# Causal phase attention on one core: all-pairs score tiles against diagonal tiles with a running state for the first 128 keys

## The reference, cut to what matters

```python
key_ph = jnp.exp(1j * key_phase).reshape(Bx, Lx, N_SETS, PLANES)
qry_ph = jnp.exp(1j * query_phase).reshape(Bx, Lx, N_SETS, PLANES)
for s in range(N_SETS):
    bound = key_ph[:, :, s, :, None] * V[:, :, None, :]
    memory = jnp.cumsum(bound, axis=1)
    retrieved = (memory * jnp.conj(qry_ph[:, :, s, :, None])).sum(axis=2).real
    total = total + weights[s] * retrieved
```

## Time and profile before

| | us |
|---|---|
| median of 3 runs | 1647.76 (1645.76 to 1649.63) |
| the profiled execution's own time | 1646.93 |
| span of the profiled execution, first to last instruction | 1644.2 |
| PE busy in the span | 1455.5 (89%) |
| DVE busy | 1432.7 (87%) |
| ACT busy | 1246.3 (76%) |
| POOL busy | 1012.6 (62%) |

### The profile page before, as it was taken

How to read it: one execution, slowest core, us unless ns; L and a number is a source line. 1 busy time by engine, 2 the same in 40 slices (tenths; PEclk the granted TensorE clock), 3 DMA queues, 4 the chain that set the end, 5 groups by cost and what they waited for, 6 DMA issues and landing times.

```text
span 1644.2 us, 30506 instructions
## 1 busy us (share of the span) xinstructions
PE 1455.5 (89%) x9030; PEld 1121.5 (68%) x9030; DVE 1432.7 (87%) x5763; ACT 1246.3 (76%) x2190; POOL 1012.6 (62%) x857
## 2 busy tenths in 40 slices
PE   2689999999999999999999999999999972776671
PEld 1467777777777777777777777777777751555551
DVE  3369999999999999999999999999999983886661
ACT  2799999999999999999999999999999741111110
POOL 0116666666666666666666666666666665788887
PEclk9899999999999999999999999999999996998885
DMA  9977777777777777777677777777776102676653
GB/s 170 245 157 151 147 145 145 141 143 133 129 124 127 123 121 120 121 123 116 120 120 120 117 117 119 119 121 121 117 119 113 39 19 65 101 117 105 94 82 34
DMA packets 257947, 195.67 MB, mean 119 GB/s; under 512 B 59000, under 2 KB 237275, under 8 KB 257784
## 3 DMA queue, kind: packets, MB, share of 16 engines
q1 hardware_dynamic: 216280, 175.30, 59.6%
q0 software_dynamic: 39296, 17.55, 8.7%
q10 hardware_dynamic: 2208, 0.89, 0.4%
HBM read 84.28 MB, written 83.73 MB: 102 GB/s over the span
## 4 chain that ended last, share of the span: by engine, by line
PE 75%; POOL 10%; issue 5%; DVE 4%; DMA 3%; ACT 3%; SPq 1%; POOLq 0%; DVEq 0%
PE bank L896 12%; POOL out_rows L640 9%; PE bank L966 8%; PE bank L949 7%; PE bank L1037 6%; PE bank L1046 5%; PE bank L920 5%; PE bank L934 4%; PE bank L904 4%; PE bank L1053 3%; PE bank L1022 2%; PE bank L985 2%; PE bank L1012 2%; PE bank L1008 2%; PE bank L1002 2%
## 5 line engine op out<-in xcount | busy, mean ns | idle before, releaser
L596 POOL DMA_INDIRECT slot_rows<-xs,slot x640 | 648.9, 1014 | 447.4 <-DVE slot L1382 278.0
L657 ACT ACTIVATE img<-img 84x980 f32<-84x980 f32 x190 | 340.5, 1793 | 13.7 <-DMA img<-in_x 7.1
L896 PE MATMUL bank<-img,w_tok 126*128 126x392 f32 (+1 forms) x640 | 228.1, 504 | 29.2 <-DMA img<-img 23.7
L640 POOL DMA_INDIRECT out_rows<-img,etok x128 | 198.7, 1552 | 54.9 <-issue 36.1
L580 POOL TENSOR_TENSOR rs<-ve,neg_half 128x12 f32<-128x12 f32 (+1 forms) x66 | 150.0, 2273 | 111.2 <-DVE ve L1265 111.2
L896 PEld LDWEIGHTS bank<-img,w_tok 126*128 126x128 f32 (+1 forms) x640 | 124.0, 195 | 115.2 <-issue 23.9
L949 PEld LDWEIGHTS bank<-pos_a,v 128*128 128x128 f32 x768 | 139.8, 190 | 42.6
L727 ACT ACTIVATE xs<-h,nb,rs 128x128 f32<-128x128 f32 x384 | 154.1, 481 | 2.5 <-DVE nb L1271 2.5
L949 PE MATMUL bank<-pos_a,v 128*128 128x325 f32 (+2 forms) x768 | 155.7, 338 | 0.0
L740 ACT ACTIVATE xh<-h,nb,rs 128x128 f32<-128x128 f32 x384 | 154.0, 480 | 0.6 <-DVE nb L1271 0.6
L966 PE MATMUL bank<-a_t,v 128*128 128x325 f32 (+2 forms) x768 | 150.3, 345 | 0.6 <-DVE a_t L1325 0.6
(11 more groups left out here) (196 smaller groups left out, 3581.6 us busy)
## 6 DMA issues: line engine op xcount, KB each, us to landing
img<-in_x SPq DMA_DIRECT2D x384, 150.1 KB
img<-img SPq DMA_DIRECT2D x254, 160.8 KB
img<-img SPq DMA_DIRECT2D x128, 128.6 KB
out_rows<-fin SPq DMA_DIRECT2D x128, 128.0 KB
slot_rows<-xs,slot POOLq DMA_INDIRECT x640
slot_rows<-init_rows SPq DMA_DIRECT2D x16, 540.0 KB, 8.9
img<-slot_rows SPq DMA_DIRECT2D x32, 270.0 KB
h<-in_txt SPq DMA_DIRECT2D x64, 128.0 KB
```

The costliest lines, as they stand in the source:

```text
L596: g.indirect_dma_start(out=slots_d, out_offset=bass.IndirectOffsetOnAxis(ap=slot[0:nt, q.x, part, r:r + 1], axis=0), in_=xs[0:nt, q.x, par ...
L640: g.indirect_dma_start(out=out, out_offset=bass.IndirectOffsetOnAxis(ap=etok[:, q.load, m:m + 1], axis=0), in_=ysum[:, q.load, m, :], in_o ...
L657: a.activation(cols[:, b0:b0 + nb, :], raw[:, q.u, :].rearrange("p (t b) -> p b t", b=P)[:, b0:b0 + nb, :], ACT.Copy)\
L896: ins = mm(bank[:, 5, 0:2 * PATCHES], w_tok[r, m, :], xk[r, k.u, :, m, :], start=(m == 0), stop=(m == SHIFT - 1))
```

## The change: what it does, and the diff

Scores are kept for the diagonal blocks and the short last one: key tile 0 against queries 0 to 127, key tile 1 against queries 128 to 324, tile 2 against queries 256 to 324, that is 128, 197 and 69 columns (394 in one bank) for 325, 197 and 69 (591 in two). What the first 128 keys give to queries 128 to 324 comes through a state: PE transposes the keys' features of both samples in one operation (`keys`, bank 7), ACT copies them to `kt` (`key_rows`), PE multiplies them with the first values tile (`first_state`, two matmuls of 128 columns with 64 output partitions each, bank 2), ACT copies the state (`state_rows`), DVE scales the queries with the norm (`scaled_queries`, 197 columns), and `phase_out` adds state times scaled queries (two matmuls of 197 columns, contraction over 64 partitions). `phase_out` is now one function for both samples. The masks become one DVE operation of 394 columns per sample. The constants grow by 394 + 197 columns.

```diff
+SCORES = [(0, TILE), (TILE, L), (2 * TILE, L)]
+AT = [0, TILE, L, L + BELOW[2]]
...
+            def key_rows(y):
+                act.wait_ge(S["pe_kt"], y.count())
+                a.activation(kt[:, :], bank[:, 7, 0:TILE], ACT.Copy).then_inc(S["a_kt"], 1)
+            def state_rows(y):
+                act.wait_ge(S["pe_st"], y.count())
+                a.activation(state[:, :], bank[:, 2, 0:D], ACT.Copy).then_inc(S["a_st"], 1)
...
                     if not early(n1, 1):
                         turn_columns_1(n1)
+                if p2.runs():
+                    key_rows(p2)
                 if p1.runs():
                     normal_1(p1)
+                if p2.runs():
+                    state_rows(p2)
                 if p3.runs():
                     normal_2(p3)
...
-            def scores(y):
+            def keys(y):
                 pe.wait_ge(S["a_qs"], y.count())
                 pe.wait_ge(S["v_w"], y.count())
+                tr(bank[:, 7, 0:TILE], kq[:, y.u, 0, 0:TILE], ident).then_inc(S["pe_kt"], 1)
+            def scores(y):
                 wait(pe, S["a_sl"], y, 2)
                 for i, (t0, _) in enumerate(TILES):
                     for s in range(2):
                         r = slice(64 * s, 64 * s + 64)
-                        b = (6, 1)[s]
-                        at = 0 if i < 2 else BELOW[1]
-                        dst = bank[:, b + (i > 0), at:at + BELOW[i]]
-                        ins = mm(dst, kq[r, y.u, 0, t0:t0 + TILE], kq[r, y.u, 1, i * TILE:L], start=(i < 2), stop=(i != 1),
-                                 skip_group_check=True)
+                        a0, a1 = SCORES[i]
+                        ins = mm(bank[:, (6, 1)[s], AT[i]:AT[i + 1]], kq[r, y.u, 0, t0:t0 + TILE], kq[r, y.u, 1, a0:a1],
+                                 start=(i == 0), stop=(i == NT - 1), skip_group_check=True)
                 ins.then_inc(S["pe_sc"], 1)
+            def first_state(y):
+                pe.wait_ge(S["a_kt"], y.count())
+                for s in range(2):
+                    ins = mm(bank[64 * s:64 * s + 64, 2, 0:D], kt[:, 64 * s:64 * s + 64], v[:, y.u, s, 0, :], start=True, stop=True)
+                ins.then_inc(S["pe_st"], 1)
...
+            def phase_out(y):
                 pe.wait_ge(S["v_ma"], y.count())
-                phase_out(y, 0)
-            def phase_out_1(y):
-                phase_out(y, 1)
+                for s in range(2):
+                    flat = a_t[:, s].rearrange("p a l -> p (a l)")
+                    for i in range(NT):
+                        a0, a1 = SCORES[i]
+                        mm(bank[:, 6 + s, a0:a1], v[:, y.u, s, i, :], flat[:, AT[i]:AT[i + 1]],
+                           start=(i == 0), stop=False, skip_group_check=True)
+                pe.wait_ge(S["a_st"], y.count())
+                for s in range(2):
+                    r = slice(64 * s, 64 * s + 64)
+                    ins = mm(bank[:, 6 + s, TILE:L], state[r, :], qn[r, :], start=False, stop=True, skip_group_check=True)
+                ins.then_inc(S["pe_ta"], 1)
...
                 pe.wait_ge(S["a_xh"], k.count())
                 wait(pe, S["v_mb"], k, 1)
+                wait(pe, S["a_st"], k, 1)
...
                 if p2.runs():
+                    keys(p2)
                     scores(p2)
                 if p4.runs():
                     counts(p4)
+                if p2.runs():
+                    first_state(p2)
+                if p4.runs():
                     shared_out(p4)
...
+            def scaled_queries(y):
+                dve.wait_ge(S["a_qs"], y.count())
+                TT(qn[:, :], kq[:, y.u, 1, TILE:L], cst("norm"), ALU.mult)
             def mask(y, s, done, b):
-                TT(a_t[:, s, 0, :], bank[:, b, 0:L], cst("maskn")[:, 0:L], ALU.mult)
-                n = BELOW[1] + BELOW[2]
-                TT(a_t[:, s, 1, 0:n], bank[:, b + 1, 0:n], cst("maskn")[:, L:], ALU.mult).then_inc(S[done], 1)
+                flat = a_t[:, s].rearrange("p a l -> p (a l)")
+                TT(flat[:, 0:AT[NT]], bank[:, b, 0:AT[NT]], cst("maskp"), ALU.mult).then_inc(S[done], 1)
...
                 if p2.runs():
                     residual_bias(p2)
+                    scaled_queries(p2)
```

More of the change, by code:

```diff
@@ L66 @@
 for _n, _w in (("ident", 128), ("pos", L), ("tok", 2 * NT), ("sel", SETS), ("query", 1), ("key", 1), ("delta", 2), ("dpos", 1),
-               ("dump", 4), ("empty", 8), ("absent", 2 * NT), ("below", 128), ("maskn", BEGIN[NT]), ("iota", CAP)):
+               ("dump", 4), ("empty", 8), ("absent", 2 * NT), ("below", 128), ("maskn", BEGIN[NT]), ("maskp", AT[NT]), ("norm", BELOW[1]),
+               ("iota", CAP)):
     CONST[_n] = (_at, _at + _w)
@@ L95, in constants @@
     put("maskn", mask * n)
+    put("maskp", np.concatenate([m0[:, 0:TILE], m1, m2], 1) * np.concatenate([invn[:, a:b] for a, b in SCORES], 1))
+    put("norm", np.repeat(invn[:, TILE:L], 128, 0))
     put("iota", np.arange(CAP)[None, :])
@@ L284, in program @@
         kq = sb("kq", [128, 2, 3, L])
+        kt = sb("kt", [128, 128])
+        state = sb("state", [128, D])
+        qn = sb("qn", [128, BELOW[1]])
         v = sb("v", [128, 2, 2, NT, D])
@@ L379, in program @@
         s_spread = [sems(f"s_spread{n}") for n in range(COPIES)]
-        names = """pe_tok pe_th pe_tx pe_k pe_v pe_g pe_sc pe_pf pe_pa0 pe_pa1 pe_ta0 pe_ta1 pe_tx2 pe_f1a  pe_lgt  pe_f3b pe_lg pe_wo pe_o
+        names = """pe_tok pe_th pe_tx pe_k pe_v pe_g pe_kt pe_st pe_sc pe_pf pe_pa0 pe_pa1 pe_ta pe_tx2 pe_f1a  pe_lgt  pe_f3b pe_lg pe_wo pe_o
             v_ht  v_st1 v_mm v_dd v_vs v_ve v_nb v_v v_ma v_mb v_w v_u v_tot v_hb  v_h2 v_st2
@@ L383, in program @@
               v_sg  v_sinv
-            a_d0 a_d1 a_d2 a_h a_xh a_xt a_th a_abs a_sin a_qs a_g a_x2 a_x2t a_lgt a_sl a_lg a_small
+            a_d0 a_d1 a_d2 a_h a_xh a_xt a_th a_abs a_sin a_kt a_st a_qs a_g a_x2 a_x2t a_lgt a_sl a_lg a_small
             p_rs""".split()
@@ L960, in position_out_1 @@
                 position_out(y, 1)
[L962 to L970, removed]
-                pe.wait_ge(S["v_ma"], y.count())
-                phase_out(y, 0)
-            def phase_out_1(y):
-                phase_out(y, 1)
+            def phase_out(y):
+                pe.wait_ge(S["v_ma"], y.count())
+                for s in range(2):
[9 more added lines that the diff above has]
+                ins.then_inc(S["pe_ta"], 1)
             def transpose_2(z):
@@ L1089, in body @@
                 if p2.runs():
-                    phase_out_0(p2)
-                    phase_out_1(p2)
+                    phase_out(p2)
                 if p3.runs():
@@ L1396, in weigh_sets @@
             def weigh_sets(y):
-                dve.wait_ge(S["pe_ta1"], y.count())
+                dve.wait_ge(S["pe_ta"], y.count())
                 STT(gsets[:, :, :], gt[:, :, :], 1.0, bank[:, 6:8, 0:L], ALU.add, ALU.mult).then_inc(S["v_u"], 1)
```

## The result

The changed kernel takes 1674.78 us (median of 4, 1673.06 to 1676.72) against 1647.65 (median of 4 on the same chip): ratio 1.0165, 95% interval 1.0147 to 1.0182. It is slower by 1.65%; the forecast was 1673 us, range 1653 to 1688.

A forecast was written before the change was run, and what follows sets the result against it. PE's list was taken to bound the kernel at 20.00 us a turn; the five items sum to +0.41, so 1646.93 + 60 x 0.41 + 1 = 1672.5, forecast 1673 us with the median's offset, range 1653 to 1688.

The forecast's parts named there:

- PE is the ring: In the loop over pairs, PE's own list sets the 20.00 us turn; time added there counts about 60 times.
- Items 1 and 2: PE, per turn: key transpose of 128 columns +0.11 us; two score pair passes cut from 325 to 128 columns, -0.33.
- Item 3: PE, first_state: two pair passes of 128 columns, 0.22 us, in a new column-half block with edges 0.36; +0.58 a turn.
- Items 4 and 5: PE, phase_out: values times masked scores shortened, -0.65 us; state times queries in a new row-half block, +0.70 a turn.
- The loads in the open: At edges of half-array blocks on PE, weight loads start with their matmuls, not ahead; counted within the new edges' 0.73 us.
- rival A: New half-array blocks' weight loads are hidden, only emptying is paid: +0.03 us a turn, 1651 us; chance 0.08.
- Rival B: PE enters and leaves half-array blocks without emptying, only streaming counts: -0.32 us a turn, 1630 us; chance 0.07.
- Other engines: ACT's two copies, estimated 0.5 us, hidden by its waits for PE; DVE's products fall from 1.81 to 1.47 us, worth nothing.
- Rival C: New ACT wait at key_rows delays transpose_1 beyond 0.6 us to spare; 0.4 beyond gives +0.81 a turn, 1697 us; chance 0.06.
- Startup: Second constants DMA grows by 295.5 KB and delays the first images by 0 to 1.5 us; taken as 1 us.

The follow-up runs named there:

- third and fourth experiments: Changed kernel, order only: key transpose moved between score products, 1695.19 us; separately, first_state moved from behind the counts to right behind the scores, 1661.30 us.
- the reordered kernel: Changed kernel reordered: key transpose between token products, first_state right ahead of scores, state products right behind them, both copies on ACT; 1660.06 us, 1.0071 of the kernel before.

## Why the prediction was right

Steps by their place in the prediction:

- *PE is the ring.* Right. The turn grew from 20.00 to 20.42, forecast +0.41, while DVE's work got shorter and ACT's waits for PE stayed near 1.2 us a turn. The order-only runs (transpose inside the scores, `first_state` behind the scores) moved the time by +0.32 and -0.23 us a turn with every engine's work unchanged.
- *Items 1 and 2* (transpose, shorter scores): -0.18 for -0.22. *Item 3* (`first_state`): 0.57 for 0.58. *Items 4 and 5* together: +0.03 for +0.05. Prices read from existing blocks of the same operand shape carried over to blocks that the trace of before doesn't have.
- *The loads in the open.* The loads of L966 and L1005 start with their matmuls, and the sum with them in the open came out; rival A is out. The Trainium skill, "TensorE: Matmul & The Clock Gate", Part 2, has weight loads pulled ahead of running matmuls when they go to the background buffer or to other rows; the trace agrees in packed work (0.11 us ahead at L1000) and doesn't where the array's division changes (730.03 for 730.04, 734.46 for both). Rival B, beside which the prediction named the span model of the Trainium skill's "TensorE: Matmul & The Clock Gate", Part 3, is out by the third and fourth experiments (0.32 and 0.23 us for edges alone). The Trainium skill's "TensorEngine Tiling (Array Packing)", Key Properties, says that a change of tiling mode drains TensorE; these two runs agree.
- *Other engines.* Right: the masks took 0.557 us of DVE for 394 columns, the scaled queries 0.359 (forecast 0.56 and 0.35); the key copy on ACT started at 728.75, the state copy ended at 731.49, 0.79 us ahead of `transpose_1` at 732.28 (forecast 0.6). Rival C did not occur. DVE's busy time fell by 0.15 us a turn, less than these lengths give (0.34); it was worth nothing, as forecast. One reading was wrong without harm: the prediction took ACT's ring as its busy time, 18.75 + 0.5 us a turn, but a stretch of PE's list is part of that ring: it closes at 19.58 us without the copies and stopped the reordered kernel at 20.17. By it rival B's turn of some 19.7 could not have been reached with the copies on ACT.
- *Startup, forecast 1 us.* Wrong; no cost shows. The token products of the sixth and the last pair in the changed kernel:

```profile
132.68 3.46 PE L918 MATMUL bank<-img,w_tok 126*128 126x392 f32 x10
...
1318.11 3.46 PE L918 MATMUL bank<-img,w_tok 126*128 126x392 f32 x10
```

Before they stood at 132.46 and 1293.01. So with the larger constants the sixth pair is 0.2 us later (the DMA still landed in 12.1, and the first token products came 1.3 us earlier), 58 turns of 0.43 make 24.9, and from the last token products to the end are 353.2 us for 351.2, 2.0 that I had not foreseen. 0.2 + 24.9 + 2.0 = 27.1 is the difference of the spans. The 2.0 can't be put down to the change: the run with `first_state` behind the scores, which has the same work, took 350.9 us there, and the seven experiments lie between 350.3 and 354.4. That the total came so near the forecast is in part luck; the turn, 0.42 for 0.41, is not, though its parts missed by 0.04, 0.01 and 0.02 in directions that nearly cancel.

## What to carry to other kernels

On a packed PE count edges before columns: where matmuls on half of the array stand alone between full-array work, read what such a block loses at entry and exit from an existing one, and add it for each new block. Small half-array groups belong side by side, whatever their place in the arithmetic. When the order is made better, look for the next ring at once: here a cycle through ACT, and then one copy that ended 0.06 us before the products that waited for it.

## What the runs showed of the hardware that I had not expected

- A product of few columns hurts its successor: behind a pass of 69 columns the next pass starts only when its weights are in, so a 197-column pass took 0.22 us for 0.165 in the run with state products on the whole array, and this without any change of the array's division.
- Two ACT copies of 64 partitions each cost far more than one of 128: in the run with padded states the list advanced 0.56 us for the two (716.70 to 717.26), in the changed kernel 0.16 us for one (731.23 to 731.39). Each half takes as long as the whole (0.27 and 0.26 us), and the operation behind it starts only after its end, where the one behind the whole copy starts 0.10 ahead of it. The 32-partition operations of `weighted_halves` do the same (0.57 us long, 0.58 apart). Why is open.
